# A four-layer graph network on one core: reflections with one matrix product each, a search by leading minors, and 26 of 62 reflections beside the first layer

## What is computed

```
h = max(layernorm(x), 0); x = x + L0(h, adj)   # A_hat h, @W1.T, batchnorm, relu, @W2.T, batchnorm
h = max(layernorm(x), 0); x = x + L1(h, adj)   # two mixes relu(adj (h W + b)), then LSTMs over windows of 1, 2, 3, 4 nodes
h = max(layernorm(x), 0); x = x + L2(h, adj)   # _, U = eigh(L_norm); U relu(U.T h W1 + b1) W2 ...
h = max(layernorm(x), 0); x = x + L3(h, adj)   # three products with adj*adj between W1, W2, W3
```

## Time and profile before

| | us |
|---|---|
| median of the runs | 1024.05 (1023.99 to 1024.16) |
| the profiled execution | 1024.09 |
| its span in the profile | 1022.3 |
| PE busy / DVE busy / ACT busy / POOL busy | 861.4 / 591.2 / 527.1 / 333.1 |
| L0 until L1's first mix product on PE | 203.8 |
| L1 until its last addition to X ends | 686.1 |
| L2's first statistics on DVE | 694.6 |

### The profile page before, as it was taken

The page is one execution under the profiler, slowest core; times in us unless marked ns, Lnnn a source line. Parts: engine busy times, 40 slices in busy tenths (PEclk is TensorE's granted clock), DMA queues, the critical chain, the costliest instruction groups (busy, mean ns, idle before and its releaser), DMA issues.

```text
span 1022.3 us, 12192 instructions
## 1 busy us (share of the span) xinstructions
PE 861.4 (84%) x3721; PEld 569.7 (56%) x3721; DVE 591.2 (58%) x2897; ACT 527.1 (52%) x962; POOL 333.1 (33%) x404
## 2 busy tenths in 40 slices
PE   2678578298979999799877989966899999999998
PEld 1444333274557645575455834754747847847856
DVE  5899867775746777468999498964404304304101
ACT  1466365276464655647546575524544544544531
POOL 1333110006656066552756357741301101101000
PEclk9998879589999999999999999987899999999999
DMA  7000000000000000000000000000000100100101
GB/s 325 0 2 0 1 0 1 1 1 1 0 1 1 1 0 2 1 1 0 1 0 1 1 1 1 1 0 1 1 1 1 42 1 1 42 0 1 43 1 41
DMA packets 2961, 13.26 MB, mean 13 GB/s; under 512 B 464, under 2 KB 464, under 8 KB 2640
## 3 DMA queue, kind: packets, MB, share of 16 engines
q1 hardware_dynamic: 2896, 12.49, 3.1%
HBM read 8.30 MB, written 4.19 MB: 12 GB/s over the span
## 4 chain that ended last, share of the span: by engine, by line
PE 55%; DVE 27%; POOL 8%; ACT 7%; issue 3%; DMA 0%; SPq 0%; DVEq 0%; ACTq 0%; POOLq 0%
PE PS L390 54%; POOL BIG L853 7%; ACT T L756 2%; DVE ST L1361 2%; ACT BIG L795 1%; DVE stats L1333 1%; DVE Fq L1170 1%; DVE Fq L1167 1%; DVE PS L1119 1%; ACT BIG L787 1%; DVE sc L1050 1%; ACT BIG L772 1%; DVE vcol L1047 1%; DVE T L1457 1%; DVE PS L1123 1%
## 5 line engine op out<-in xcount | busy, mean ns | idle before, releaser
L390 PE MATMUL PS<-BIG,wts 128*128 128x512 f32 (+2 forms) x1264 | 438.1, 500 | 37.6 <-POOL BIG L853 21.8
L390 PEld LDWEIGHTS PS<-BIG,wts 128*128 128x128 f32 x1264 | 239.9, 195 | 198.1 <-issue 112.7
L853 POOL TENSOR_TENSOR BIG<-BIG 128x256 f32<-128x256 f32 (+2 forms) x272 | 254.8, 943 | 247.8 <-ACT BIG L787 183.0
L787 ACT ACTIVATE BIG<-PS,lbias 128x256 f32<-128x256 f32 (+2 forms) x312 | 165.2, 558 | 102.6 <-PE PS L390 102.0
L694 ACT ACTIVATE BIG<-PS 128x1024 f32<-128x1024 f32 x64 | 65.5, 1023 | 88.9 <-PE PS L390 88.9
L694 ACT ACTIVATE T<-PS 128x512 f32<-128x512 f32 x96 | 55.1, 593 | 98.6 <-PE PS L390 98.6
L702 ACT ACTIVATE T<-X,shift,rstd 128x128 f32<-128x128 f32 x192 | 78.3, 482 | 52.4 <-DVE shift L1349 52.4
L1472 DVE TENSOR_TENSOR X<-X,PS 128x512 f32<-128x512 f32 x64 | 43.4, 682 | 107.1 <-PE PS L390 87.1
L390 PE MATMUL PS<-T,wts 128*128 128x512 f32 x192 | 100.3, 653 | 1.0 <-ACT T L694 0.7
L1493 DVE TENSOR_TENSOR T<-PS,wts 128x512 f32<-128x512 f32 x16 | 11.1, 691 | 150.9 <-PE PS L390 150.9
L841 POOL TENSOR_SCALAR rstd<-mv 128x4 f32<-128x4 f32 x48 | 10.9, 228 | 234.6 <-DVE mv L1340 234.6
(11 more groups left out here) (235 smaller groups left out, 1141.5 us busy)
## 6 DMA issues: line engine op xcount, KB each, us to landing
X<-x_in SPq DMA_DIRECT2D x1, 4096.0 KB, 12.8
out<-X SPq DMA_DIRECT2D x16, 256.0 KB, 2.0
wts<-w_in SPq DMA_DIRECT2D x1, 3605.5 KB, 21.8
cst<-cst_in SPq DMA_DIRECT2D x1, 371.0 KB, 3.2
AA<-adj_in SPq DMA_DIRECT2D x2, 16.0 KB, 2.0
```

Source lines behind the costliest of these rows:

```text
L390: return nc.tensor.matmul(o, l, r, start=start, stop=stop)
L787: nc.scalar.activation(LB[:, q, {"i": I_, "g": G_, "f": F_, "o": O_}[g], 0:n], PS[:, 3 * q + rank[q] % 3, 0:n], ACT.Tanh if g == "g" else ...
L853: nc.gpsimd.tensor_tensor(out, a, b, op).then_inc(pool_set[q], 1)
```

## The change

What it does, in the order of the program:

- **One meeting for a reflection.** `row_product` goes. Row k+1 of the matrix before update k comes from a product with the identity (`old_row`) that PE sends together with the `av_product` of reflection k; DVE forms the updated row itself (`xrow`, and for own roots a copy in PSUM), and the two instructions that update S are put into the waits of the next reflection (`update`, `aside`). With POOL's root a reflection is 23 DVE instructions instead of 16, with the own root 34 instead of 24.
- **26 reflections beside L0 in place of 31.** L0 keeps its 31 steps; the last five have none. 36 stand beside L1. The second batchnorm's scales now wait for DVE's own counts of the chunks.
- **Search by leading minors** in two rounds in place of three. The first spreads 4096 points over all 128 lanes, the second 64. A step has four combinations of 128 x 32 (`scalar_tensor_tensor`) and no reciprocal, and there is one rescaling on the way. The end has two reciprocals, a comparison of 2048 and one of 2016 elements per lane, and a tree of additions of 1024 to 32; the first round adds a comparison and a reduction of 2048.
- **Twist as one recurrence.** Lanes 0 to 63 go forward and 64 to 127 backward, two instructions of 128 x 1 a step over 64 steps, three rescalings of six. Then reciprocals and clamps, and one more PE product joins both ways (`both_ways`).
- **The planner's numbers** follow.

```diff
-PACE = 2.5
-PACE_ROW = 1.8
-PACE_AV = 4.9
-PACE_GRID = 38.0
-PACE_TWIST = 45.0
+PACE = 3.0
+PACE_AV = 8.0
+PACE_GRID = [40.0, 32.0]
+PACE_TWIST = 27.0
+PACE_SCAN = 13.0
...
-            def row_product(k):
-
-                pe.wait_ge(hh_x, k + 1)
...
+            def old_row(o, k):
+
+                n = NODES - 1 - k
+                return mm(o[:, 0:n], ident[0:NODES, k:k + 1].broadcast_to((NODES, P)), S[0:NODES, k + 1:NODES])
 
             def av_product(k):
 
                 pe.wait_ge(hh_v, k + 1)
+                if k + 1 < REFLECTIONS:
+                    old_row(eb(3), k + 1)
...
-                row_product(r)
...
-                av_product(r)
+                if r < REFLECTED:
+                    av_product(r)
...
+            def update(k, in_psum):
+                trail = S[:, k + 1:NODES]
+                z = (eb(1) if in_psum else zrow)[:, 0:NODES - 1 - k]
+                first = op(v.scalar_tensor_tensor(trail, z, vn, trail, ALU.mult, ALU.add))
+                yield
+                dve.wait_ge(hh_ops, first)
+                op(v.scalar_tensor_tensor(trail, row_of(k, in_psum), zn, trail, ALU.mult, ALU.add))
+                yield
...
-                        gop(v.reciprocal(rq[:, 0, :], Qh[:, i, :]))
...
-                    gop(v.tensor_reduce(cnt[:, :], Qh[:, :, :].rearrange("p i m -> p m i"), AX, ALU.add))
+                    gop(v.tensor_tensor(Z[:, 0:NODES - 1, :], Z[:, 0:NODES - 1, :], Z[:, 1:NODES, :], ALU.not_equal))
...
+                for i in range(NODES):
+
+                    s, j = divmod(i, 16)
+                    at = seg[:, s, j + 1:j + 2]
+                    if i < NODES - 1:
+                        top_op(v.tensor_scalar(t2[:, i + 1:i + 2], at, ne2d[:, i:i + 1], None, ALU.mult))
+                    top_op(v.tensor_scalar(seg[:, s, j + 2:j + 3], at, ad[:, i:i + 1], t2[:, i:i + 1] if i else 0.0,
+                                           ALU.mult, ALU.add))
+                    top_sync()
...
-            for r in range(REFLECTED):
+            first_row()
+            for r in range(L0_STEPS):
...
-                reflection(r, True, beside)
+                if r < REFLECTED:
+                    reflection(r, True, beside)
                 for _ in beside:
                     pass
+            for k in range(NK):
+                dve.wait_ge(dve_done[k], B_DVE.end)
```

More of the change, by code:

```diff
@@ L41 @@
 M = 32
-ROUNDS = 3
+ROUNDS = 2
 REFLECTIONS = NODES - 2
@@ new lines, in reflection @@
+                need(op(v.tensor_scalar(beta, sg, -1.0, norm, ALU.add, ALU.mult)), beside)
+                op(v.tensor_scalar(vcol[:, :], C("next")[:, k:k + 1], beta, xc, ALU.mult, ALU.add))
+                if not by_pool:
+                    op(v.tensor_scalar(vr[:, 0:1], vr[:, 0:1], beta, None, ALU.add))
+                got = op(v.tensor_scalar(x0, x0, beta, None, ALU.add))
+                need(got, beside)
+                v.tensor_tensor_reduce(junks[:, 3, 0:m], trail, vr, 1.0, 0.0, ALU.mult, ALU.add, S[:, NODES:NODES + 1])\
+                    .then_inc(hh_v, 1)
@@ new lines, in tail, with gop, gsync @@
+                step(v.tensor_scalar(s1(1), s1(0), 1.0001, TINY, ALU.mult, ALU.add))
+                step(v.tensor_scalar(s1(2), s1(1), -2.0 / (P * M + 1), None, ALU.mult), "bound")
+                xn, ta, tb, cn = (eb(1)[:, n * M:(n + 1) * M] for n in range(4))
+                g = [0]
+                def gop(ins):
+                    g[0] += 1
+                    ins.then_inc(grid_ops, 1)
+                def gsync(back=0):
+                    beside_l1()
+                    dve.wait_ge(grid_ops, g[0] - back)
@@ L1172, in tail @@
-                dve.wait_ge(twist_ops, 4 * (NODES - 1))
-                step(v.tensor_tensor(gam, top, bot, ALU.add))
-                step(v.tensor_tensor(gam, gam, a, ALU.subtract))
+                low, high = slice(0, NODES), slice(NODES, P)
+                ratio, inv, a, gam, hot, zt, zb, mul, t2 = (Fq[:, n, :] for n in range(9))
+                rows = ratio.rearrange("p (s j) -> p s j", s=4)
+                irows = inv.rearrange("p (s j) -> p s j", s=4)
+                step(v.tensor_copy(Tdir[:, :, :], Trow[:, 1:4, :]))
@@ new lines, in tail @@
+                step(v.tensor_copy(Tdir[high, 0, :], Trow[high, 1, ::-1]))
+                step(v.tensor_copy(Tdir[high, 1:3, 0:NODES - 1], Trow[high, 2:4, NODES - 2::-1]))
+                step(v.memset(seg[:, 0, :], 0.0))
+                step(v.memset(seg[:, 0, 1:2], 1.0))
+                step(v.memset(both_ways[:, :], 0.0))
+                ad, ne2d, ned = (Tdir[:, n, :] for n in range(3))
+                step(v.tensor_scalar(a, d, s1(1), None, ALU.add))
+                step(v.tensor_scalar(ad, ad, s1(1), None, ALU.add))
@@ new lines, in tail @@
+                step(v.reciprocal(rows, seg[:, :, 1:17]))
+                step(v.reciprocal(irows, seg[:, :, 2:18]))
+                step(v.tensor_tensor(rows, rows, seg[:, :, 2:18], ALU.mult))
+                step(v.tensor_tensor(irows, irows, seg[:, :, 1:17], ALU.mult))
+                step(v.tensor_scalar(both_ways[low, 0:NODES], ratio[low, :], 1e18, -1e18, ALU.min, ALU.max))
+                step(v.tensor_scalar(both_ways[high, 0:NODES], ratio[high, ::-1], 1e18, -1e18, ALU.min, ALU.max))
```

367 lines of the change are left out of this document (214 added, 153 removed).

## The result

The changed kernel takes 1051.81 us (1045.68 to 1056.11), the kernel before 1024.06 (1023.99 to 1024.16): ratio 1.0266, 95% interval 1.0203 to 1.033. It is slower, as forecast, but by 28 us and not by 10. Its four runs scatter by 10 us, those of the kernel before by 0.2 (by up to 4.2 us where it was measured 18 times). The profiled execution took 1055.64 us, its span is 1053.7.

What follows compares the result with a forecast made beforehand. DVE was taken to bound L0's first pass and PE's chain of LSTM products L1. L0 +8 and L1 +1.7 gave +9.7 on the profiled 1024.09 us: 1034 us, own range 1028 to 1040, whole range 1014 to 1043.

Steps and rivals of the forecast that it cites:

- First pass of L0: L0's first pass: seven more DVE instructions per reflection, +1.0 for twelve full steps, +0.6 for nine others; +17.4 us.
- Second pass: L0's second pass: five steps lose their reflection (-6.6) and the second batchnorm's scales come earlier (-3.1); -9.7 us.
- The twist: L1, fold to join: DVE needs 37.8 us at 0.44 a step, PE's products 26.2; PE waits 11.6.
- rival (c): End of the search's second round: POOL and DVE block each other at the shared port; +5 to +8, 1040; chance 0.13.
- The second fold: L1, end of the search's second round: DVE ready at 613, PE at 605.7; wait 7.4, loss +6.
- What goes: L1: 15.0 us of PE's old waits for DVE and the 8.5 us tail disappear; -23.5 together.
- +6.9 for the reflections: L1's reflections: ten more small PE products (+3.3) and DVE late at three narrow gaps (+3.6).
- The tail: End of L1: the 8.5 us of decomposition between L1's last addition and L2's first statistics go.
- my +1.7: L1 behind the join: V's transpose comes 12.4 us later, DVE needs about 14; +1.7.
- Rival (a): Places fit and L1 gains, with a twist step of 0.28 to 0.30: 1018 or 1012; chance 0.27 together with (d).
- (b): Both kernels even: twist at 0.30, L0 its full +8, fold +6; 1024.1 within 2; chance 0.08.
- Rival (d): L0's first pass isn't bound by DVE, so the seven instructions fit: 1022; chance 0.27 together with (a).

Runs made afterwards that it cites:

- e3: Changed kernel with only the join's place later (PACE_TWIST 41 in place of 27): 1038.15 us, ratio 1.0137.
- e10: Changed kernel with all places of the search and twist later (PACE_GRID 40 and 38, PACE_TWIST 41, PACE_SCAN 14): 1034.23 us, ratio 1.0106.
- e15: Changed kernel with e9's reflections, e11's DVE-list clock in the search alone, 0.30 in the twist, and places for both: 1025.53 us, ratio 1.0038.
- e9: Changed kernel with reflections closer and search earlier (PACE_AV 7.0, PACE_GRID 54 and 46, PACE_TWIST 41, PACE_SCAN 15): 1028.10 us, ratio 1.0054.
- e11: e9 with DVE_STEP 0.17 in place of 0.24 and the search's long instructions added to the planner's DVE clock: 1029.40 us, ratio 1.0067.
- e13: Changed kernel with PACE_AV 7.4, PACE_GRID 45 and 42, PACE_TWIST 41, PACE_SCAN 15 and e11's DVE-list clock: 1040.53 us, ratio 1.0163.
- e12: Changed kernel with e11's planner clock for DVE's list and nothing else: 1046.33 us, ratio 1.0221.

## Why the prediction was right or wrong, point by point

- **First pass of L0, +17.4: right in kind, small.** The full step grew by 1.0 as worked out (6.25 for 5.25). The pass grew by 21: two steps of 7.4 and 7.2 us fell into a stretch at the lower clock (0.50 in the window 60:75), where the kernel before has 1.00. Together they are 2 of the 3.6 us; what lowered the clock there wasn't found. I had taken the clock as given.
- **Second pass, -9.7: too small.** It gave back 15.6 (from +21.1 at the first reflection of the pass to +5.5 at the second batchnorm's relu; the scales came at 188.94, where some 191 was expected). Steps without a reflection took 4.0 us, not 4.3, and those with one 5.4, not 5.6.
- **The twist, 11.6: right in the step, and the wait in part by luck.** 0.43 a step for 0.44, 12.1 us of wait; e3 confirms the wait by taking it away. A dependent pair was the right reading, and the earlier trace rows with the earlier trace rows were enough for it. But from fold to join DVE took 39.8 us and not 37.8, since the three rescalings took 6.3 and not 3.4 (rival (c) below says why), and PE's 28 products took 27.7 and not 26.2.
- **The second fold: the wait was right (8.2 for 7.4), by errors that nearly cancelled.** The comparison of 2016 took 3.20 us and the first steps of the tree 3.00, not some 1.3 each; the row that I had used, has one SBUF input and these have two. 0.9 of the 3.20 is rival (c). From its last bias DVE took 24.0 us and not 21.6, but PE came 9.7 us later than the 605.7 of the forecast and the bias only 8.0 later. The loss was 11.4 and not 6: PE's wait for POOL in front of it stayed (2.06), and the clock fell (0.81 between the products at 588.4 and 612.6, where the kernel before has 1.00).
- **"What goes", -23.5: this is the step that failed, for 17 of the missing 22 us.** It counted each microsecond of old wait, and the tail, as a microsecond of L1's time, and that was wrong in two places.
  - *Up to the last iteration* -11.5 of it (4.6, 3.9 and 3.0), with +6.9 for the reflections, were to make -4.6; measured is +2.9. The waits did go: those of PE for DVE fell from 12.5 us to 5.5 between the products at 203.8 and 588.4. The time did not follow. PE's waits for POOL grew from 19.1 us to 23.0 and those for ACT from 22.3 to 24.8, and PE was busy for 341.5 us in place of 337.5, with 16 more records of small products and a granted clock of 0.938 in place of 0.965. Some 3 us of the difference of 7.5 may be scatter: e10 has the same lists up to here and measured -0.1.
  - *The tail* of 8.5 went from behind L1, but into it: its dependent small products moved in among the LSTMs, where PE takes its list in order and stood still for DVE at three of them (3.0, 1.2 and 2.6 us). 14.8 us were lost there for 15.2 that came back at L1's end, against my +1.7 and about -12, a difference of 9.9. From the product at 636.7 to that at 701.3 both kernels take the same time, 64.5 us before and 64.1 after. I had priced V's meeting in the new place and not those behind it, nor the products themselves.
- **The rest of the 22 us**: the fold 5.4 more than forecast, the join 2.2, the 1.0 that POOL and ACT were to catch up; against it L0 2.9 less and 1.4 back in L2.
- **What the slower time is not.** It is not DVE's work in L1. e15 has the same instructions and takes 26 us less. Of the 28 us, 26 are the places of the products and the order of DVE's list. What is left in e15's trace is +5.5 in L0, -3.1 in L1 and -1.4 in L2: +1.1.
- **Rival (a)** (places fit, 1012 to 1018) needed a twist of 0.29 a step; it was 0.43, and (b) fell with it. Its sum doesn't come out either: 0.29 takes 9.6 us off the wait at the join and the shorter end 2 off that at the fold, which leaves 7 us of wait and not 2, so about 1022. With better places (e15) L1 gained 3. **Rival (d)** fell with the step of 6.25. **Rival (c)** is a real mechanism of small size: in e9, with POOL at work, and in e11, with POOL idle, the same two instructions of DVE:

```profile
599.78 1.23 DVE L1218 TENSOR_SCALAR Z<-Z 128x2048 f32<-128x2048 f32 x1
601.04 3.21 DVE L1220 TENSOR_TENSOR Z<-Z 128x2016 f32<-128x2016 f32 x1
```

```profile
594.34 1.23 DVE L1218 TENSOR_SCALAR Z<-Z 128x2048 f32<-128x2048 f32 x1
595.60 2.26 DVE L1221 TENSOR_TENSOR Z<-Z 128x2016 f32<-128x2016 f32 x1
```

and POOL in e9 beside them (two instructions in 5.28, then two in 3.13), against the changed kernel's two in 2.49 where DVE has no such instruction:

```profile
600.09 5.28 POOL L873 TENSOR_TENSOR BIG<-BIG 128x512 f32<-128x512 f32 x2 [0.74 <-ACT BIG L814]
606.11 3.13 POOL L873 TENSOR_TENSOR BIG<-BIG 128x512 f32<-128x512 f32 x2 [0.74 <-ACT BIG L814]
```

```profile
607.16 2.49 POOL L873 TENSOR_TENSOR BIG<-BIG 128x512 f32<-128x512 f32 x2 [0.74 <-ACT BIG L814]
```

It costs 1 us on DVE and 3 on POOL here. The instruction of 128x2048, of one input, is the same in both; in e9 it started 0.31 us before POOL's. But an input alone doesn't decide it. In the changed kernel's twist the same small instruction of one input, on 128 x 2, takes 1.32 us beside POOL and 0.23 with POOL idle:

```profile
634.28 1.32 DVE L1293 TENSOR_SCALAR seg<-seg,sc 128x2 f32<-128x2 f32 x1
...
653.34 0.23 DVE L1293 TENSOR_SCALAR seg<-seg,sc 128x2 f32<-128x2 f32 x1
```

```profile
634.30 1.27 POOL L873 TENSOR_TENSOR BIG<-BIG 128x512 f32<-128x512 f32 x1 [1.02 <-ACT BIG L806]
```

Two more instructions of the second rescaling, at 643 to 645 us, take 1.15 and 1.13 us beside POOL, so this adds 3.0 us to the twist. With the fold's 0.9 rival (c) is 4 us of DVE's time in the changed kernel, ahead of two products for which PE waits. The Trainium skill, page "SBUF — State Buffer", section "SBUF: two separate sides", says of a DVE instruction with two SBUF inputs, or in a 2-port mode, that it and a GpSimd instruction exclude each other, and that the one that starts later waits. The rows with two inputs agree that the two engines hold each other up; in which mode the instructions of one input ran, the one of 1.92 us in the earlier trace rows among them, no row says.

## What to carry to other kernels

Where one engine takes its list in order, work that is made shorter elsewhere gives nothing until the places in both lists are set again: find them by where the trace of the new kernel has each operand ready, and look at both engines' waits, since a wait of DVE for PE (12.3 us in e9) can be the cause of PE's wait for DVE 30 us later. Moving a chain of dependent small steps from behind a stage into it hides the chain only if each meeting is hidden, so price every one of them, and don't count a wait that goes as time that goes: here waits for DVE fell by 7.0 us and the stretch didn't get shorter, since waits for the other engines grew by 6.4. A change that lengthens a part bound by DVE by 1 us a step to shorten a part with idle time must gain that back there first; here, in no kernel that was tried did the 17 us in L0 pay.

## What the runs showed of the hardware that I had not expected

Kernels with the same instructions differ by several microseconds, and not in one place alone. Eleven traces have the new form with 26 reflections; ten reach L1 at +4.1 to +6.7 us, and e13 at +10.9. The changed kernel and e10, the same up to the second fold, differ by 0.9 us in L0 and by another 3.0 in L1 ahead of 588.4.

e12 and e13 ran the same L0. Their rows of 80:120 are equal in clock (0.68) and in PE's busy time (31.99). They part behind it; the windows view of 120:135, e12 and then e13:

```profile
120.00:135.00 15.00, 11.06 (x47) 6.52 (x46) 12.57 (x77) 7.23 (x13) 2.33 (x4) 0.93 0.00 1
```

```profile
120.00:135.00 15.00, 12.83 (x42) 7.21 (x41) 10.94 (x65) 6.52 (x12) 2.06 (x3) 0.70 0.00 1
```

The clock is 0.93 in one and 0.70 in the other, PE is busy longer with fewer products, and DVE, which sets the pace, waits more; e13 reaches L1 4.2 us later than e12. So in these two traces a step of L0 feels a fall of the clock. Why the clock differs was not found. In 80:120 it is 0.87 in e10 and the changed kernel, 0.74 in e11, and 0.68 in e12 and e13; the three that are lower ran on one chip, where the kernel before was as fast as on the others (1023.8 us). The new form scatters more than the old (10.6 us over ten runs of e15, 4.2 over eighteen of the kernel before). With one meeting in place of two PE stands on the chain of a step with its slow product too; that this is the reason was not tried.
